# Running the first half of the wide matmul ahead of the small projection, and storing from GpSimd instead of ScalarE

## The chip, the cores and the metric

The kernel runs on one Trainium2 chip, on 8 cores. Each core handles one batch element of the input on its own: no data passes between cores. The metric is the device time of the slowest core in microseconds (us), lower is better.

## The reference, cut to what matters

For each batch element `x` is 4096 x 2048 in float32. `S` is 64.

```
xn = layernorm(x)                                # per row of 2048
a  = tanh(xn @ Wa.T + ba);  b = tanh(xn @ Wb.T + bb)      # 4096 x 64 each
h_t = a_t * h_(t-1) + b_t                        # scan over the 4096 rows
attn = xn + hs @ Wout.T + bout
scale = mean(|weight|)
w_t   = clip(round(weight / scale), -1, 1)       # 2048 x 2048, three values
ffn   = xn @ (w_t * scale).T + bias
y     = x + attn + ffn
```

## The kernel before, in words

A first stage (until about 174 us) prepares the weights. It loads the 2048 x 2048 matrix once to find its scale and again to make its three-valued form, turned by TensorE into `w_rhs` in bfloat16, and turns the two small projections into `wab` (128 columns: 64 for a, 64 for b).

Then comes the main loop over `NT` = 32 tiles of 128 rows, which has all that the change touches. There is no planner; each engine has a program written out by hand and meets the others by semaphores only. Buffers of a tile (`sx`, `xnb`, `xnT`, `outb`, `vv`) are doubled, but the accumulator `pffn` (128 x 2048 in float32, filled in four parts of 512 columns), the transpose buffer `ptr` and the small accumulator `pab` are single. For tile k:

- TensorE (the `tensor` block) computes `pab`: one bias matmul (L510) and 16 matmuls of 128 columns (L515). The first 8 need the first half of `xnT` and the last 8 its second half. It then waits until the first half of `pffn` of tile k-1 has been evicted (`s_ev` at 2k-1) and runs 32 matmuls of 512 columns for the first half of `pffn` (L527, L530). After `s_ev` at 2k it runs 32 more for the second half (L538, L542). Next are 16 transposes of tile k+1 from `xnb` into `ptr` (L552, L557), and four matmuls of `hsbe` with `wocv` that add the recurrent part to `pffn` (L566 to L572, below called the mix). The second and the fourth of the mix release the two evictions by `s_mix`.
- ScalarE (`scalar`) waits for both evictions of tile k-1 (`s_ev` at 2k) and issues the store of its `outb` (L263). It waits for `pab`, applies tanh to its two halves (L271, L272), makes `xnb` of tile k+1 (L281), scales the scan's result into `hsbe` (L290), and copies the transposes in two halves from `ptr` to `xnT` (L299, L303). The last store is L307.
- VectorE (`vector`) runs the scan (L394), copies its last column, makes the sums and sums of squares of tile k+2 (L371, L373), evicts the two halves of `pffn` into `outb` (L405, L411), and makes `vv` of tile k+1 (L421). L405 also waits for the store that last read its `outb` buffer, that of tile k-2.
- GpSimd (`gpsimd`, POOL in the rows) runs `chain(j)` for each tile: some twenty small operations (L601 to L633) that turn the sums into the row's scale and shift, `s_stats`, released by the drain of L635.
- SyncE (`sync`) loads `sx` of tile k+2 (L192) when `xnb` and `vv` of tile k have been made from it.

The order on TensorE around the change, as the code has it:

```python
                for c in range(NCH):
                    if c == 8:
                        tensor.wait_ge(s_xnT, 2 * k + 2)
                    ins = tensor.matmul(pab[:, :],
...
                ins.then_inc(s_ab, 1)
                if k == 0:
                    tensor.wait_ge(s_wtrc, 32)
                else:
                    tensor.wait_ge(s_ev, 2 * k - 1)
```

Of the kernel before, what the change touches and what calls it, by code (L numbers as in the profile page):

```python
# [15 lines left out]
T, D, S = 4096, 2048, 64  # L16
TT = 128
NT = T // TT
NCH = D // 128
# [6 lines left out]
def build():  # L26
# [12 lines left out]
    y_d = nc.dram_tensor("y", [T, D], F32, kind="ExternalOutput").ap()  # L39

    with ExitStack() as est:
# [9 lines left out]
        wab = sb("wab", [128, NCH * 128], BF16)  # L51
        wocv = sb("wocv", [65, D], BF16)
        hsbe = sb("hsbe", [65, TT], BF16)
        babr = sb("babr", [1, 128], BF16)
        sidn = sb("sidn", [128, 128], BF16)
        sonr = sb("sonr", [1, 128], BF16)
        sx = sb("sx", [128, 2 * D], F32)
        xnb = sb("xnb", [128, 2 * D], BF16)
        xnT = sb("xnT", [128, 2 * D], BF16)
        outb = sb("outb", [128, 2 * D], F32)  # L60
# [46 lines left out]
        pab = e(nc.psum_tensor("pab", [128, 128], F32))  # L107
        spare = e(nc.psum_tensor("spare", [128, 512], F32))
        s_x0, s_x1 = sem("s_x0"), sem("s_x1")
        s_st0, s_st1 = sem("s_st0"), sem("s_st1")  # L110
# [7 lines left out]
        s_small = sem("s_small")  # L118
# [5 lines left out]
        s_wabcp = sem("s_wabcp")  # L124
        s_bab = sem("s_bab")
# [71 lines left out]
        def _(scalar):  # L197
# [60 lines left out]
            scalar.drain()  # L258
            scalar.copy(xnT[:, 1024:2048], ptr[:, 1024:2048]).then_inc(s_xnT, 1)
            for k in range(NT):  # L260
                if k >= 1:
                    scalar.wait_ge(s_ev, 2 * k)
                    scalar.dma_start(  # L263
                        out=y_d[128 * (k - 1):128 * k, :],
                        in_=outb[:, ((k - 1) % 2) * D:((k - 1) % 2 + 1) * D]
                    ).then_inc(s_st[(k - 1) % 2], 16)
                scalar.wait_ge(s_ab, k + 1)
                if k >= 1:
                    scalar.wait_ge(s_scan, k)
                scalar.drain()  # L270
                scalar.activation(sa[:, :], pab[0:64, :], AF.Tanh)  # L271
                scalar.activation(sb0[:, :], pab[64:128, :], AF.Tanh  # L272
                                  ).then_inc(s_tanh, 2)
                if k < NT - 1:
                    j = k + 1
                    jsl = j % 2
                    scalar.wait_ge(s_stats, j + 1)
                    if k >= 1:
                        scalar.wait_ge(s_tr, 2 * k)
                    scalar.drain()  # L280
                    scalar.activation(xnb[:, jsl * D:(jsl + 1) * D],  # L281
                                      sx[:, jsl * D:(jsl + 1) * D], AF.Identity,
                                      bias=nmr[:, jsl:jsl + 1],
                                      scale=yr[:, jsl:jsl + 1]
                                      ).then_inc(s_xnbs, 1)
                scalar.wait_ge(s_scan, k + 1)
                if k >= 1:
                    scalar.wait_ge(s_mix, 2 * k)
                scalar.drain()
                scalar.activation(hsbe[0:64, :], hs[:, :], AF.Identity,  # L290
                                  bias=0.0, scale=invs64[:, :]).then_inc(s_hsb, 1)
                if k < NT - 1:
                    j = k + 1
                    jsl = j % 2
                    scalar.wait_ge(s_tr, 2 * k + 3)
                    if k >= 1:
                        scalar.wait_ge(s_ffn, k)
                    scalar.drain()
                    scalar.copy(xnT[:, jsl * D:jsl * D + 1024],  # L299
                                ptr[:, 0:1024]).then_inc(s_xnT, 1)  # L300
                    scalar.wait_ge(s_tr, 2 * k + 4)
                    scalar.drain()  # L302
                    scalar.copy(xnT[:, jsl * D + 1024:jsl * D + 2048],  # L303
                                ptr[:, 1024:2048]).then_inc(s_xnT, 1)

            scalar.wait_ge(s_ev, 2 * NT)
            scalar.dma_start(  # L307
                out=y_d[128 * (NT - 1):128 * NT, :],
                in_=outb[:, ((NT - 1) % 2) * D:((NT - 1) % 2 + 1) * D]
            ).then_inc(s_st[(NT - 1) % 2], 16)  # L310
            scalar.wait_ge(s_st0, 16 * ((NT + 1) // 2))
            scalar.wait_ge(s_st1, 16 * (NT // 2))

        @block.vector
        def _(vector):
# [112 lines left out]
        def _(tensor):  # L428
# [71 lines left out]
            for k in range(NT):  # L500
                ksl = k % 2
                xo = ksl * D
                if k >= 1:
                    tensor.wait_ge(s_tanh, 2 * k)
                else:
                    tensor.wait_ge(s_bab, 1)
                    tensor.wait_ge(s_wabcp, 2)
                    tensor.wait_ge(s_small, N_SMALL)
                tensor.wait_ge(s_xnT, 2 * k + 1)
                tensor.matmul(pab[:, :], babr[:, :], sonr[:, :],  # L510
                              start=True, stop=False)
                for c in range(NCH):
                    if c == 8:
                        tensor.wait_ge(s_xnT, 2 * k + 2)
                    ins = tensor.matmul(pab[:, :],  # L515
                                        wab[:, 128 * c:128 * (c + 1)],
                                        xnT[:, xo + 128 * c:xo + 128 * (c + 1)],
                                        start=False, stop=(c == NCH - 1))
                ins.then_inc(s_ab, 1)
                if k == 0:  # L520
                    tensor.wait_ge(s_wtrc, 32)
                else:
                    tensor.wait_ge(s_ev, 2 * k - 1)
                for c in range(NCH):
                    st_ = (c == 0)
                    lhs = xnT[:, xo + 128 * c:xo + 128 * (c + 1)]
                    tensor.matmul(pffn[:, 0:512],  # L527
                                  lhs, w_rhs[:, 2048 * c:2048 * c + 512],
                                  start=st_, stop=False)
                    tensor.matmul(pffn[:, 512:1024],  # L530
                                  lhs, w_rhs[:, 2048 * c + 512:2048 * c + 1024],
                                  start=st_, stop=False)
                if k >= 1:
                    tensor.wait_ge(s_ev, 2 * k)
                for c in range(NCH):
                    st_ = (c == 0)
                    lhs = xnT[:, xo + 128 * c:xo + 128 * (c + 1)]
                    tensor.matmul(pffn[:, 1024:1536],  # L538
                                  lhs,
                                  w_rhs[:, 2048 * c + 1024:2048 * c + 1536],  # L540
                                  start=st_, stop=False)
                    ins = tensor.matmul(  # L542
                        pffn[:, 1536:2048], lhs,
                        w_rhs[:, 2048 * c + 1536:2048 * c + 2048],
                        start=st_, stop=False)
                ins.then_inc(s_ffn, 1)
                if k < NT - 1:
                    j = k + 1
                    jo = (j % 2) * D
                    tensor.wait_ge(s_xnbs, j + 1)  # L550
                    for c in range(8):
                        ins = tensor.transpose(  # L552
                            ptr[:, 128 * c:128 * (c + 1)],
                            xnb[:, jo + 128 * c:jo + 128 * (c + 1)], sidn[:, :])
                    ins.then_inc(s_tr, 1)
                    for c in range(8, 16):
                        ins = tensor.transpose(  # L557
                            ptr[:, 128 * c:128 * (c + 1)],
                            xnb[:, jo + 128 * c:jo + 128 * (c + 1)], sidn[:, :])
                    ins.then_inc(s_tr, 1)  # L560
                tensor.wait_ge(s_hsb, k + 1)
                if k == 0:
                    tensor.wait_ge(s_wocp, 1)
                    tensor.wait_ge(s_cvr, 16 * 16)
                    tensor.wait_ge(s_hrow, 1)
                tensor.matmul(pffn[:, 0:512], hsbe[:, :], wocv[:, 0:512],  # L566
                              start=False, stop=True)
                tensor.matmul(pffn[:, 512:1024], hsbe[:, :], wocv[:, 512:1024],  # L568
                              start=False, stop=True).then_inc(s_mix, 1)
                tensor.matmul(pffn[:, 1024:1536], hsbe[:, :], wocv[:, 1024:1536],  # L570
                              start=False, stop=True)
                tensor.matmul(pffn[:, 1536:2048], hsbe[:, :], wocv[:, 1536:2048],  # L572
                              start=False, stop=True).then_inc(s_mix, 1)

        @block.gpsimd
        def _(g):
# [59 lines left out]

            chain(0)
            chain(1)
            for k in range(2, NT):
                chain(k)  # L640
            g.wait_ge(s_st0, 16 * ((NT + 1) // 2))
            g.wait_ge(s_st1, 16 * (NT // 2))

# [30 lines left out]
```

## Time and profile before

| what | us |
|---|---|
| median of the runs (2 runs, 739.09 to 740.08) | 739.59 |
| the profiled execution, its own time | 739.52 |
| its span, slowest core (core 5) | 737.9 |
| spans of the other cores | 732.8 to 736.9 |
| TensorE busy in the span | 590.1 |
| VectorE, ScalarE, GpSimd busy | 348.9, 235.9, 195.0 |

The span runs from the first to the last instruction of a core; the execution's own time is 1.6 us longer than the slowest span. Matmuls are pipelined: a matmul of 512 columns is shown as 0.38 us long but the next begins 0.22 us after it, so TensorE is read by the distance from one start to another. "PEld" is the loading of a matmul's fixed operand, which goes on beside the matmul before it. The suffix q (ACTq, SPq, POOLq) means an engine's queue of instructions that are not computation, such as the issue of a DMA.

### The profile page before, as it was taken

What the parts mean: (1) busy time and instruction counts of PE and PEld (TensorE: products, weight loads), DVE (VectorE), ACT (ScalarE), POOL (GpSimd) and SP (SyncE); (2) the same over time, 40 slices, a digit from 0 to 9 for tenths busy, and PEclk for the clock granted to TensorE, in tenths of its full rate; (3) what the DMA queues carried; (4) which work ended last, traced back from release to release, by engine and by line L of the source; (5) the groups of instructions that cost most, each with busy time, mean ns of one, the idle gap of its engine ahead of it and who ended that gap; (6) DMA issues with size and microseconds to landing.
All of it is one profiled execution on the core that took longest, in us unless ns stands there. A gap on an engine that the chain in (4) does not pass through costs nothing.

```text
span 737.9 us, 11312 instructions; the slowest of 8 cores (732.8 to 737.9 us)
## 1 busy us (share of the span) xinstructions
PE 590.1 (80%) x3804; PEld 312.0 (42%) x3804; DVE 348.9 (47%) x303; ACT 235.9 (32%) x250; POOL 195.0 (26%) x710
## 2 busy tenths in 40 slices
PE   0021244435999999999999999999999999999996
PEld 0021234323444444445444444444444445444442
DVE  0000099982344455554555554444455555555521
ACT  1275444533223222222332322233222222332320
POOL 1000022354222222222333333322222222323310
PEclk9999999999999999999999999999999999999998
DMA  8979557711244333333333344344333333333321
GB/s 231 297 234 334 189 170 258 258 56 58 69 129 139 123 115 115 115 115 115 115 115 114 124 138 137 126 133 136 122 116 114 115 115 115 115 115 115 122 84 81
DMA packets 17072, 103.03 MB, mean 140 GB/s; under 512 B 4566, under 2 KB 4598, under 8 KB 4598
## 3 DMA queue, kind: packets, MB, share of 16 engines
q1 hardware_dynamic: 9590, 51.96, 22.4%
q10 hardware_dynamic: 4608, 33.56, 12.7%
q0 software_dynamic: 2816, 16.78, 6.9%
q8 instruction: 31, 0.51, 0.3%
q14 instruction: 27, 0.22, 0.1%
HBM read 68.73 MB, written 33.55 MB: 139 GB/s over the span
## 4 chain that ended last, share of the span: by engine, by line
PE 64%; DMA 9%; ACT 8%; DVE 4%; DVEq 4%; ACTq 4%; issue 3%; SPq 2%; POOLq 1%; POOL 0%
PE pffn L527 15%; PE pffn L530 15%; PE pffn L538 15%; PE pffn L542 15%; ACT xnT L303 4%; DMA wtile<-wf 4%; DVE wbn L359 3%; ACTq L302 3%; PE pab L515 3%; DMA outb<-wf 2%; DMA wasb<-wb 2%; PE ptr L552 2%; DVEq L358 2%; SPq L171 2%; ACT xnT L232 2%
## 5 line engine op out<-in xcount | busy, mean ns | idle before, releaser
L527 PE MATMUL pffn<-w_rhs,xnT 128*128 128x512 bf16 x512 | 194.7, 380 | 0.6 <-DVE outb L405 0.6
L530 PE MATMUL pffn<-w_rhs,xnT 128*128 128x512 bf16 x512 | 194.6, 380 | 0.0
L538 PE MATMUL pffn<-w_rhs,xnT 128*128 128x512 bf16 x512 | 194.0, 379 | 0.0
L542 PE MATMUL pffn<-w_rhs,xnT 128*128 128x512 bf16 x512 | 194.0, 379 | 0.0
L371 DVE TENSOR_REDUCE sums<-sx 128x1 f32<-128x2048 f32 x32 | 73.2, 2286 | 191.0 <-DMA sx<-x 190.8
L281 ACT ACTIVATE xnb<-sx,nmr,yr 128x2048 bf16<-128x2048 f32 x31 | 65.0, 2097 | 106.8 <-POOLq L635 106.7
L299 ACT COPY xnT<-ptr 128x1024 bf16<-128x1024 bf16 x31 | 31.4, 1013 | 203.3 <-PE ptr L552 203.3
L601 POOL TENSOR_SCALAR mm_<-sums 128x1 f32<-128x1 f32 x32 | 9.6, 300 | 286.9 <-DVE sqscr L373 278.6
L542 PEld LDWEIGHTS pffn<-w_rhs,xnT 128*128 128x128 bf16 x512 | 50.1, 98 | 60.4
L538 PEld LDWEIGHTS pffn<-w_rhs,xnT 128*128 128x128 bf16 x512 | 50.1, 98 | 60.4
L405 DVE SCALAR_TENSOR_TENSOR outb<-pffn,negs,vv 128x1024 f32<-128x1024 f32 x32 | 41.1, 1284 | 72.4 <-PE pffn L568 72.4
L527 PEld LDWEIGHTS pffn<-w_rhs,xnT 128*128 128x128 bf16 x512 | 50.2, 98 | 57.7 <-issue 1.4
L530 PEld LDWEIGHTS pffn<-w_rhs,xnT 128*128 128x128 bf16 x512 | 50.2, 98 | 57.0 <-issue 0.6
L373 DVE SCALAR_TENSOR_TENSOR sqscr<-sx 128x2048 f32<-128x2048 f32 x32 | 73.0, 2281 | 0.0
L485 PE MATMUL ptr<-sidn,wbn 128*128 128x128 bf16 x256 | 29.8, 309 | 35.4 <-DVE wbn L359 35.4
L515 PE MATMUL pab<-xnT,wab 128*128 128x128 bf16 x512 | 40.0, 222 | 10.1 <-ACT xnT L303 10.1
L421 DVE TENSOR_SCALAR vv<-sx,p1r,nmr 128x2048 f32<-128x2048 f32 x31 | 41.7, 1347 | 3.0
L243 ACT COPY w_rhs<-ptr 128x1024 bf16<-128x1024 bf16 x32 | 32.4, 1013 | 33.5 <-PE ptr L485 32.1
L485 PEld LDWEIGHTS ptr<-sidn,wbn 128*128 128x128 bf16 x256 | 26.0, 144 | 39.5 <-issue 39.5
L411 DVE SCALAR_TENSOR_TENSOR outb<-pffn,negs,vv 128x1024 f32<-128x1024 f32 x32 | 41.1, 1284 | 3.0
L585 POOL DMA_DIRECT2D outb<-wf x11 | 10.3, 932 | 118.2 <-DVE wbn L359 117.7
L454 PE MATMUL spare<-onescolb,xnT 128*128 128x1 bf16 x256 | 9.0, 165 | 39.1 <-ACT xnT L232 39.1
(100 smaller groups left out, 562.3 us busy)
## 6 DMA issues: line engine op xcount, KB each, us to landing
sx<-x SPq DMA_DIRECT2D x32, 1024.0 KB, 6.9
y<-outb ACTq DMA_DIRECT2D x32, 1024.0 KB, 5.2
outb<-wf POOLq DMA_DIRECT2D x11, 1024.0 KB, 7.1
wtile<-wf SPq DMA_DIRECT2D x8, 1024.0 KB, 11.0
vv<-wf SPq DMA_DIRECT2D x8, 1024.0 KB, 10.5
sqscr<-wf POOLq DMA_DIRECT2D x5, 1024.0 KB, 7.3
wasb<-wa SPq DMA_DIRECT2D x1, 512.0 KB
wosb<-wout SPq DMA_DIRECT2D x16, 32.0 KB, 10.3
```

The costliest lines, as they stand in the source:

```text
L281: scalar.activation(xnb[:, jsl * D:(jsl + 1) * D], sx[:, jsl * D:(jsl + 1) * D], AF.Identity, bias=nmr[:, jsl:jsl + 1], scale=yr[:, jsl:js ...
L371: vector.reduce_sum(sums[:, jsl:jsl + 1], sx[:, jsl * D:(jsl + 1) * D], axis=AX.X)
L373: vector.scalar_tensor_tensor(sqscr[:, :], sx[:, jsl * D:(jsl + 1) * D], 1.0, sx[:, jsl * D:(jsl + 1) * D], OP.mult, OP.mult, accum_out=sq ...
L405: vector.scalar_tensor_tensor(outb[:, ksl * D:ksl * D + 1024], pffn[:, 0:1024], negs128[:, :], vv[:, ksl * D:ksl * D + 1024], OP.mult, OP. ...
L411: vector.scalar_tensor_tensor(outb[:, ksl * D + 1024:ksl * D + 2048], pffn[:, 1024:2048], negs128[:, :], vv[:, ksl * D + 1024:ksl * D + 2048],
L421: vector.tensor_scalar(vv[:, jsl * D:(jsl + 1) * D], sx[:, jsl * D:(jsl + 1) * D], p1r[:, jsl:jsl + 1], nmr[:, jsl:jsl + 1], OP.mult, OP.a ...
L485: ins = tensor.transpose(ptr[:, 128 * c:128 * (c + 1)], wbn[:, sl * D + 128 * c:sl * D + 128 * (c + 1)], sidn[:, :])
L515: ins = tensor.matmul(pab[:, :], wab[:, 128 * c:128 * (c + 1)], xnT[:, xo + 128 * c:xo + 128 * (c + 1)], start=False, stop=(c == NCH - 1))
L527: tensor.matmul(pffn[:, 0:512], lhs, w_rhs[:, 2048 * c:2048 * c + 512], start=st_, stop=False)
L530: tensor.matmul(pffn[:, 512:1024], lhs, w_rhs[:, 2048 * c + 512:2048 * c + 1024], start=st_, stop=False)
L538: tensor.matmul(pffn[:, 1024:1536], lhs, w_rhs[:, 2048 * c + 1024:2048 * c + 1536], start=st_, stop=False)
L542: ins = tensor.matmul(pffn[:, 1536:2048], lhs, w_rhs[:, 2048 * c + 1536:2048 * c + 2048], start=st_, stop=False)
```

## The change

Three edits in the main loop.

1. On TensorE the 32 matmuls for the first half of `pffn` go ahead of the 17 for `pab`. The wait for the eviction (`s_ev` at 2k-1) and that for `xnT` now stand before these 32, and the wait for the second half of `xnT` is at their channel 8. The 17 of `pab` come between the first and the second half of `pffn`.
2. ScalarE no longer waits for the evictions and no longer issues the stores, nor does it wait for them at the end.
3. GpSimd issues them: after `chain(k + 2)` it waits for both evictions of tile k and issues the store of tile k.

```diff
@@ scalar
             for k in range(NT):
-                if k >= 1:
-                    scalar.wait_ge(s_ev, 2 * k)
-                    scalar.dma_start(
-                        out=y_d[128 * (k - 1):128 * k, :],
-                        in_=outb[:, ((k - 1) % 2) * D:((k - 1) % 2 + 1) * D]
-                    ).then_inc(s_st[(k - 1) % 2], 16)
                 scalar.wait_ge(s_ab, k + 1)
...
-            scalar.wait_ge(s_ev, 2 * NT)
-            scalar.dma_start(
-                out=y_d[128 * (NT - 1):128 * NT, :],
-                in_=outb[:, ((NT - 1) % 2) * D:((NT - 1) % 2 + 1) * D]
-            ).then_inc(s_st[(NT - 1) % 2], 16)
-            scalar.wait_ge(s_st0, 16 * ((NT + 1) // 2))
-            scalar.wait_ge(s_st1, 16 * (NT // 2))
@@ tensor
-                if k >= 1:
-                    tensor.wait_ge(s_tanh, 2 * k)
-                else:
-                    tensor.wait_ge(s_bab, 1)
-                    tensor.wait_ge(s_wabcp, 2)
-                    tensor.wait_ge(s_small, N_SMALL)
-                tensor.wait_ge(s_xnT, 2 * k + 1)
-                tensor.matmul(pab[:, :], babr[:, :], sonr[:, :],
-                              start=True, stop=False)
-                for c in range(NCH):
-                    if c == 8:
-                        tensor.wait_ge(s_xnT, 2 * k + 2)
-                    ins = tensor.matmul(pab[:, :],
-                                        wab[:, 128 * c:128 * (c + 1)],
-                                        xnT[:, xo + 128 * c:xo + 128 * (c + 1)],
-                                        start=False, stop=(c == NCH - 1))
-                ins.then_inc(s_ab, 1)
                 if k == 0:
                     tensor.wait_ge(s_wtrc, 32)
                 else:
                     tensor.wait_ge(s_ev, 2 * k - 1)
+                tensor.wait_ge(s_xnT, 2 * k + 1)
                 for c in range(NCH):
+                    if c == 8:
+                        tensor.wait_ge(s_xnT, 2 * k + 2)
...
+                if k >= 1:
+                    tensor.wait_ge(s_tanh, 2 * k)
+                else:
+                    tensor.wait_ge(s_bab, 1)
+                    tensor.wait_ge(s_wabcp, 2)
+                    tensor.wait_ge(s_small, N_SMALL)
+                tensor.matmul(pab[:, :], babr[:, :], sonr[:, :],
+                              start=True, stop=False)
+                for c in range(NCH):
+                    ins = tensor.matmul(pab[:, :],
+                                        wab[:, 128 * c:128 * (c + 1)],
+                                        xnT[:, xo + 128 * c:xo + 128 * (c + 1)],
+                                        start=False, stop=(c == NCH - 1))
+                ins.then_inc(s_ab, 1)
                 if k >= 1:
                     tensor.wait_ge(s_ev, 2 * k)
@@ gpsimd
             chain(0)
             chain(1)
-            for k in range(2, NT):
-                chain(k)
+            for k in range(NT):
+                if k < NT - 2:
+                    chain(k + 2)
+                ksl = k % 2
+                g.wait_ge(s_ev, 2 * k + 2)
+                g.dma_start(out=y_d[128 * k:128 * (k + 1), :],
+                            in_=outb[:, ksl * D:(ksl + 1) * D]
+                            ).then_inc(s_st[ksl], 16)
```

## Rows read from the trace of the kernel before

**Rows 1.** Spans and granted TensorE clock of the cores.
```profile
core 5: 737.9 us, clock 0.997
```

**Rows 2.** The page's busy times, and TensorE in 40 slices of the span.
```profile
PE 590.1 (80%) x3804; PEld 312.0 (42%) x3804; DVE 348.9 (47%) x303; ACT 235.9 (32%) x250; POOL 195.0 (26%) x710
...
PE   0021244435999999999999999999999999999996
```

**Rows 3.** Waits, whole span: engine line <- releaser: us in total, times, longest.
```profile
PE pab L515 <- ACT xnT L303: 10.1, 31, 0.3
```

**Rows 4.** Timeline, boundary from tile 18 to 19: start us, us, engine, line, operation [idle before].
```profile
505.22 0.61 PE L552 MATMUL ptr<-sidn,xnb 128*128 128x128 bf16 x8
...
506.02 1.01 ACT L299 COPY xnT<-ptr 128x1024 bf16<-128x1024 bf16 x1 [6.70 <-PE ptr L552]
...
506.33 0.38 PE L568 MATMUL pffn<-wocv,hsbe 65*128 65x512 bf16 x1
...
506.93 1.28 DVE L405 SCALAR_TENSOR_TENSOR outb<-pffn,negs,vv 128x1024 f32<-128x1024 f32 x1 [1.93 <-PE pffn L568]
...
507.18 0.21 PE L510 MATMUL pab<-sonr,babr 1*128 1x128 bf16 x1
...
507.32 0.62 PE L515 MATMUL pab<-xnT,wab 128*128 128x128 bf16 x8
...
508.26 0.61 PE L515 MATMUL pab<-xnT,wab 128*128 128x128 bf16 x8 [0.33 <-ACT xnT L303]
...
508.71 0.38 PE L527 MATMUL pffn<-w_rhs,xnT 128*128 128x512 bf16 x1
```

**Rows 5.** Timeline, one tile later: the same transposes.
```profile
522.52 0.61 PE L552 MATMUL ptr<-sidn,xnb 128*128 128x128 bf16 x8
```

**Rows 6.** Timeline, an earlier boundary, where the eviction came late.
```profile
265.06 1.28 DVE L405 SCALAR_TENSOR_TENSOR outb<-pffn,negs,vv 128x1024 f32<-128x1024 f32 x1
...
266.49 0.38 PE L527 MATMUL pffn<-w_rhs,xnT 128*128 128x512 bf16 x1 [0.57 <-DVE outb L405]
```

**Rows 7.** Timeline, the other engines about the boundary of rows 4.
```profile
500.50 2.29 DVE L371 TENSOR_REDUCE sums<-sx 128x1 f32<-128x2048 f32 x1 [5.97 <-DMA sx<-x]
...
505.64 0.22 POOL L601 TENSOR_SCALAR mm_<-sums 128x1 f32<-128x1 f32 x1 [9.14 <-DVE sqscr L373]
...
509.67 0.34 ACTq L263 DMA_DIRECT2D y<-outb  x1
509.69 1.35 DVE L421 TENSOR_SCALAR vv<-sx,p1r,nmr 128x2048 f32<-128x2048 f32 x1
...
510.21 0.27 ACT L271 ACTIVATE sa<-pab 64x128 f32<-64x128 f32 x1 [2.10 <-DVE outb L411]
...
511.12 0.33 SPq L192 DMA_DIRECT2D sx<-x  x1
511.13 0.48 DVE L394 TENSOR_TENSOR_SCAN hs<-sa,h_in,sb 64x128 f32<-64x128 f32 x1
...
513.62 0.19 POOL L633 TENSOR_TENSOR nmr<-mm_,yr 128x1 f32<-128x1 f32 x1
...
514.04 2.10 ACT L281 ACTIVATE xnb<-sx,nmr,yr 128x2048 bf16<-128x2048 f32 x1 [3.27 <-POOLq L635]
```

**Rows 8.** Loads of sx (L192): us from issue to landing.
```profile
DMA to landing us min/median/max: 6.3/6.9/9.0
```

**Rows 9.** Weight loads of the small projection, 300 to 730 us: busy, mean ns.
```profile
L515 PEld LDWEIGHTS pab<-xnT,wab 128*128 128x128 bf16 x395 | 22.6, 97 | 13.6 <-issue 11.7
```

**Rows 10.** The tail, and GpSimd's own DMA issues (ns min/median/max) and landings.
```profile
733.71 0.34 ACTq L307 DMA_DIRECT2D y<-outb  x1
...
L585 POOL DMA_DIRECT2D outb<-wf x11: 528/947/1525, 1.7 to 144.4; - x11
...
DMA to landing us min/median/max: 6.4/7.1/14.1
```

**Rows 11.** Timeline of TensorE at tile 0, after a long idle time.
```profile
176.64 1.91 PE L515 MATMUL pab<-xnT,wab 128*128 128x128 bf16 x16
```

## The prediction, made before the change was run

> **What bounds the kernel now.** I read the spans first: the slowest core is core 5, at full TensorE clock [rows 1], and the others are alike, so one core tells all. The busy times and the slices come next: TensorE is at 9 tenths in every slice of the main loop and nothing else is near it [rows 2]. The question is thus only what TensorE does in one tile and where it stands still. The transposes of two successive tiles start at 505.22 and 522.52 [rows 4, 5]: a period of 17.30 us. Of that, from 508.71 to 522.52, 13.81 us go to the 64 wide matmuls, 0.216 each without a hole. The rest, from 505.22 to 508.71, is the boundary: 3.49 us. I read the boundary in the timeline, since all that the change moves ends there.
>
> In the boundary [rows 4] the 16 transposes and two matmuls of the mix are started by 506.33. That releases the eviction L405 (506.93 to 508.21). Beside it ScalarE copies the transposes (L299 from 506.02 to 507.03, then L303). The bias matmul L510 starts 0.15 us after the first copy ends, the first 8 of `pab` at 507.32; the next 8 wait 0.33 us for the second copy and start at 508.26. The waits show this 31 times, 10.1 us in total [rows 3]. The wide matmuls start at 508.71, when `pab` is through. The eviction had then been done for 0.5 us. So today the 17 matmuls of `pab` are what fills TensorE while it could not start the wide ones anyway: all but the last stretch of them lies in the shadow of L405.
>
> **TensorE: the wide half first.** What it saves is the start of the wide matmuls. They now need the first half of `xnT` (507.03) and the eviction L405 (508.21). The eviction is later and so it decides. How long after it TensorE starts is shown at one earlier boundary, where the eviction happened to be late: L405 from 265.06, so until 266.34, and the first wide matmul at 266.49 [rows 6]: 0.15 us. After the change the wide matmuls thus start at 508.36 in place of 508.71. Saved: 0.35 us for each boundary. Their channel 8 comes 16 matmuls or 3.4 us later, long after the second copy, so that wait costs nothing.
>
> What it costs: the 17 matmuls of `pab` no longer lie in a wait but in the stream of wide ones, with TensorE already full. In a stream they take their distance from one start to the next: from 508.26 to 508.71 eight of them take 0.45 us, 0.056 each [rows 4]. The 16 transposes with as many columns take the same (505.22 to about 506.11, when the mix begins 0.22 before L568). So 17 x 0.056 = 0.96 us. The lower bound is 0.94 (0.89 us for 16 transposes, scaled to 17); the upper is 1.05, if the bias matmul keeps the 0.14 us between it and the next (507.18 to 507.32) in place of 0.056. I take 0.96, as its weight load can go beside the wide matmul ahead of it.
>
> In sum for each boundary: 0.96 - 0.35 = +0.61 us, between 0.56 (0.94, and 0.03 us less delay after the eviction) and 0.70. The period becomes 17.91. There are 31 boundaries: +18.9 us, between 17.4 and 21.7. At tile 0 there is no eviction to wait for, and before and after TensorE does the same matmuls without a hole: 0. At the one boundary of rows 6 the eviction alone held the wide matmuls back, by about 0.4 us; with the better cover computed below that goes: -0.4 us.
>
> The page "TensorE: Matmul & The Clock Gate" of the Trainium skill (section "Back-to-back issue gap") puts matmuls of 128 columns, each with a weight load, at about 81 ns sustained rather than 56. By it the block would be an estimated 1.38 us and the whole some 13 us slower than my sum. This trace has 56 ns for just these matmuls [rows 4], and I go by it.
>
> **What gets late by it.** I count from the first wide matmul of a tile, t = 0, so that the eviction L405 before it ends at -0.15. `pab` is now complete at about t = 6.9 + 0.96 + 0.17 = 8.0 rather than before 0. Before, L271 started 2.10 us late, behind the eviction and the store issue, and the scan came 0.92 us after it (510.21 and 511.13) [rows 7]; now tanh starts at about 8.2 and the scan at 9.1 to 9.6, its column copy by 9.9. `xnb` of the next tile waited for GpSimd's chain (at 514.04, t = 5.3) and now for tanh: 8.8 to 10.9, and `hsbe` to 11.4. The transposes need `xnb` at 14.8 and the mix needs `hsbe` at 15.7. Both are covered, by 3.9 and 4.3 us.
>
> On VectorE the sums start when `sx` has landed or the scan is done. Load: L421 ends 511.04 and SyncE issues at 511.12 [rows 7], which in the new count is t = 2.76; at the median landing of 6.9 us [rows 8] that is 9.7, against 9.9 for the scan. The sums take 4.5 us and L405 follows 0.1 later. L405 is due at 14.77 (64 wide and `pab`) + 1.71 (505.22 to 506.93) = 16.5. So a landing may take up to 9.1 us, where it was 8.5 before; the longest seen is 9.0 [rows 8]. The cover of the sums becomes a little better, not worse.
>
> **Stores.** ScalarE loses its wait for both evictions and a 0.34 us issue, none of it on the path: ScalarE stood idle for 3.3 us ahead of L281 and now waits for `pab` in any case. I put it at nothing. GpSimd issues the store after the chain. The chain starts 0.64 us after the sums end and took 8.2 us (505.64 to 513.8) [rows 7], so the store is issued at about t = 5.3 of the next tile instead of 0.96. The next chain starts 0.6 us after the next sums, at about 15, so the issue (0.95 us [rows 10]) holds up nothing. The buffer is written again two tiles after its eviction, over 30 us later: nothing. Only the last store is on the path. Before, it was issued at 733.71 and the span ended at 737.9, 4.2 us. GpSimd's issue is 0.6 us longer than ScalarE's (0.947 against 0.34), and its 1 MB loads landed at best 6.4 us after issue [rows 10], but with other transfers beside them. Bounds: 0 and +2.8 (0.6, and 6.4 - 4.2). I take +1.0, nearer to the bare issue since the last store runs alone.
>
> The Trainium skill's page "DMA: Bandwidth & Descriptors" (section "Specifications") gives a first byte after about 1 us from GpSimd and 0.6 from the other queues. By it the tail would be an estimated 0.4 us longer, inside my bounds.
>
> **Sum.** Against the profiled execution's 739.5 us: +18.9 - 0.4 + 1.0 = +19.5, so 759.0 us. The median shown is 739.6, the same to 0.1. That is 2.6% slower.
>
> **Rivals.**
> A. The wide matmuls start before the eviction's time (the other side: faster). The mechanism: L405 ends ahead of the copy, so that only `xnT` at 507.03 holds TensorE. The wide matmuls then start at 507.18, a gain of 1.53 against 0.96: -0.57 for 31 boundaries, -17.7, plus the tail: 723. It decides from an L405 that ends before about 507.6 (508.71 - 0.96 - 0.15); at that point the change is worth nothing. Against it: L405 begins 0.22 after the mix matmul it needs, L568, has ended, and nothing of the change moves L568 nearer. For it I find no row. 0.02.
> B. The eviction holds less than I think, and the loss is about 0.4 a boundary: 739.5 + 31 x 0.4 + 1 = 753, within 2%. It would need the block at 0.8 us or a start 0.2 earlier. No row shows either. 0.05.
> C. The block costs more: in the stream the weight loads of `pab` are not hidden. One load takes 97 ns [rows 9]; 17 in full would be 1.65 us, +1.30 a boundary, 780. For it: the wide matmuls leave each load 216 ns, the narrow ones 56. Against it: the eight at 508.26 went at 0.056 with the same loads. 0.03. The skill's 81 ns, told above, would lie between.
> D. `sx` comes too late. The store now goes out inside the load's flight (5.3 in 2.8 to 9.7) instead of ahead of it, from a queue that shows landings of 7.1 us [rows 10]. The price is one for one beyond 9.1 us: with a median landing of 10, +0.9 x 31 = 28 us, so 787. Against it: before, a store as long as the last one (4.2) already lay beside the load for some 3 us (0.96 + 4.2 against the load's 2.4); now the load has its first 2.5 us to itself. 0.04.
> E. TensorE's clock falls in the longer hole. Its standstill at the boundary grows from two holes of 0.1 and 0.3 us to one of 1.2 us (L568 at 506.33 and two more at 0.216 and 0.38 long end at 507.14; to 508.36). After the long idle time ahead of tile 0, 16 matmuls of `pab` took 1.91 us, at the 1.2 GHz level, twice their time [rows 11]. If each boundary brought some 3 us of loss, +90: 850. No hole as long as 1.2 us lies in the main loop of before, so this stays open; the short ones that are there leave the pace untouched. 0.01.
>
> **How the numbers follow.** My forecast has 0.85. The range of its own terms is 756.5 (17.4, -0.4, 0) to 764.4 (21.7, 0.4 of rows 6 not recovered, 2.8). Taking in the edge of B and part of C, the range is 755 to 766. A measurement of this kernel tells about 2% from no change, 754.4 us here. Faster by over 2%: A, 0.02. Within 2%: B, 0.05. Slower by over 2%: 0.93.
>
> **What would show it.** In the changed kernel's timeline: the first L527 (new line) of a tile 0.15 us after L405 ends, released by VectorE in all 31 waits and no longer by ScalarE's L303; the second half's first matmul 0.96 us later than a wide matmul's pace would have it, the 17 of `pab` without a hole; transposes 17.9 us apart; L371 starting about 10 us after the first wide matmul; L405 still waiting for TensorE, not for the sums; the store issued by GpSimd about 5 us into the next tile; 5 us from the last issue to the end of the span. It is wrong if the period is below 17.75 or above 18.0, if L405 starts late behind L373, or if wide matmuls stand 0.43 us apart after a boundary.

## The result, and the profile of the changed kernel

The changed kernel takes 768.7 us (median) against 739.9 us for the kernel before on the same chips: a ratio of 1.0393, 95% interval 1.0376 to 1.041, so 3.9% slower. The forecast was slower too, but at 759.0 us with 766 as the upper end: the sign and the place are right, the size is a third too small. The profiled execution took 766.9 us, its slowest span is 765.4 us, against 739.5 and 737.9 before.

The changed kernel's page, the busy times and TensorE in slices:

```profile
PE 587.8 (77%) x3804; PEld 308.5 (40%) x3804; DVE 348.9 (46%) x303; ACT 235.6 (31%) x250; POOL 213.7 (28%) x742
...
PE   0121244409999899999999999999999998999995
```

The same work (587.8 us busy against 590.1 in [rows 2]) in a longer span: the loss is time in which TensorE stands still. The waits of the changed kernel's TensorE name it:

```profile
PE pffn L499 <- DVE outb L391: 41.1, 31, 1.4
```

L391 is the eviction of the first half (L405 before) and L499 the first wide matmul. In [rows 3] the boundary's only wait was for ScalarE's second copy, 0.33 us each, 10.1 in all, with `pab` around it. Now it is one wait of 1.3 us, 31 times, and nothing fills it. The timeline of the changed kernel from the middle of one tile to the start of the next:

```profile
504.75 0.38 PE L499 MATMUL pffn<-w_rhs,xnT 128*128 128x512 bf16 x1 [1.33 <-DVE outb L391]
...
511.44 0.38 PE L502 MATMUL pffn<-w_rhs,xnT 128*128 128x512 bf16 x1
511.75 0.22 PE L511 MATMUL pab<-sonr,babr 1*128 1x128 bf16 x1
511.91 1.07 PE L514 MATMUL pab<-xnT,wab 128*128 128x128 bf16 x16
512.81 0.38 PE L524 MATMUL pffn<-w_rhs,xnT 128*128 128x512 bf16 x1
...
519.72 0.61 PE L538 MATMUL ptr<-sidn,xnb 128*128 128x128 bf16 x8
...
520.83 0.38 PE L554 MATMUL pffn<-wocv,hsbe 65*128 65x512 bf16 x1
...
521.43 1.28 DVE L391 SCALAR_TENSOR_TENSOR outb<-pffn,negs,vv 128x1024 f32<-128x1024 f32 x1 [2.20 <-PE pffn L554]
...
522.97 0.38 PE L499 MATMUL pffn<-w_rhs,xnT 128*128 128x512 bf16 x1 [1.33 <-DVE outb L391]
```

The period is 522.97 - 504.75 = 18.22 us, where [rows 4, 5] had 17.30 and the prediction 17.91. Two places hold the missing 0.31:

- The wide matmul starts 0.26 us after the eviction has ended (521.43 + 1.28 = 522.71), not the 0.15 of [rows 6]. That is +0.11.
- From the last wide matmul of the first half, at 511.44, plus its 0.216, to the first of the second half at 512.81 `pab` takes 1.15 us, not 0.96. The 16 matmuls run at 0.056 (511.91 to 512.81), as foretold. The rest is at the one bias matmul, L511: it starts 0.31 after the wide one instead of 0.22, and the next starts 0.16 after it instead of 0.06. That is +0.19.

The weight loads about the bias matmul, in the same timeline, show how it differs from the others:

```profile
511.23 0.10 PEld L502 LDWEIGHTS pffn<-w_rhs,xnT 128*128 128x128 bf16 x1
...
511.75 0.09 PEld L511 LDWEIGHTS pab<-sonr,babr 1*128 1x128 bf16 x1 [0.42 <-issue]
...
511.90 0.90 PEld L514 LDWEIGHTS pab<-xnT,wab 128*128 128x128 bf16 x16
```

A wide matmul's load runs 0.2 us ahead of its matmul, beside the one before: the load of L502 at 511.23, the matmul at 511.44. L511's load comes only with its own matmul, and so does the first load behind it.

The whole difference adds up. From the first wide matmul of tile 1 to that of tile 31 (30 periods) it was 519.8 us before and is 546.5 now: +26.7. From there to the end of the span it was 21.6 and is 23.8: +2.2, which is the `pab` block (1.15) and the tail (+1.06). Ahead of tile 1 it is 1.4 less: this core came into the loop 0.65 earlier; tile 0 took 0.54 less (18.41 between the transposes of tile 0 and tile 1, before 18.95), which is told at the end; and the first boundary, from the transposes to the wide matmul, took 0.24 less (3.19, before 3.43). Sum +27.5, as 765.4 - 737.9.

### The profile page after: what moved, and what is told of

It is laid out like the page before. It is cut to its first block, busy times and chain, and to the rows that moved or that the text cites. A ratio compares the mean times of both kernels' runs of the same rounds, so it can differ in the third digit from the quotient of the medians.

```text
span 765.4 us, 11310 instructions; the slowest of 8 cores (761.0 to 765.4 us)
## 1 busy us (share of the span) xinstructions
PE 587.8 (77%) x3804; PEld 308.5 (40%) x3804; DVE 348.9 (46%) x303; ACT 235.6 (31%) x250; POOL 213.7 (28%) x742
## 3 DMA queue, kind: packets, MB, share of 16 engines
q0 software_dynamic: 7424, 50.34, 17.3%
## 4 chain that ended last, share of the span: by engine, by line
PE 70%; DVE 8%; DMA 7%; DVEq 5%; issue 3%; SPq 2%; ACT 2%; POOLq 1%; ACTq 1%; POOL 0%
PE pffn L499 15%; PE pffn L502 15%; PE pffn L528 14%; PE pffn L524 14%; DVE outb L391 5%; PE pab L514 4%; DMA vv<-wf 4%; DVE wbn L345 2%; DVEq L344 2%; DVEq L339 2%; PE ptr L538 2%; PE ptr L543 2%; DMA wasb<-wb 2%; SPq L171 2%; ACT xnT L232 1%
## 5 line engine op out<-in xcount | busy, mean ns | idle before, releaser
L499 PE MATMUL pffn<-w_rhs,xnT 128*128 128x512 bf16 x512 | 194.6, 380 | 41.6 <-DVE outb L391 41.1
L502 PE MATMUL pffn<-w_rhs,xnT 128*128 128x512 bf16 x512 | 194.6, 380 | 0.0
L380 DVE TENSOR_TENSOR_SCAN hs<-sa,h_in,sb 64x128 f32<-64x128 f32 x32 | 15.2, 476 | 219.8 <-ACT sb L266 219.8
L499 PEld LDWEIGHTS pffn<-w_rhs,xnT 128*128 128x128 bf16 x512 | 50.1, 98 | 113.4 <-issue 57.0
L265 ACT ACTIVATE sa<-pab 64x128 f32<-64x128 f32 x32 | 8.7, 271 | 280.7 <-PE pab L514 280.7
L391 DVE SCALAR_TENSOR_TENSOR outb<-pffn,negs,vv 128x1024 f32<-128x1024 f32 x32 | 41.1, 1284 | 77.3 <-PE pffn L554 77.3
L502 PEld LDWEIGHTS pffn<-w_rhs,xnT 128*128 128x128 bf16 x512 | 50.1, 98 | 57.1 <-issue 0.8
L611 POOL TENSOR_SCALAR t0s<-t0s 128x1 f32<-128x1 f32 x96 | 41.3, 431 | 15.3 <-issue 15.3
L571 POOL DMA_DIRECT2D outb<-wf x11 | 10.1, 920 | 117.6 <-DVE wbn L345 117.2
L397 DVE SCALAR_TENSOR_TENSOR outb<-pffn,negs,vv 128x1024 f32<-128x1024 f32 x32 | 41.1, 1284 | 3.0
```

The costliest lines, as they stand in the source:

```text
L391: vector.scalar_tensor_tensor(outb[:, ksl * D:ksl * D + 1024], pffn[:, 0:1024], negs128[:, :], vv[:, ksl * D:ksl * D + 1024], OP.mult, OP. ...
L397: vector.scalar_tensor_tensor(outb[:, ksl * D + 1024:ksl * D + 2048], pffn[:, 1024:2048], negs128[:, :], vv[:, ksl * D + 1024:ksl * D + 2048],
L499: tensor.matmul(pffn[:, 0:512], lhs, w_rhs[:, 2048 * c:2048 * c + 512], start=st_, stop=False)
L502: tensor.matmul(pffn[:, 512:1024], lhs, w_rhs[:, 2048 * c + 512:2048 * c + 1024], start=st_, stop=False)
L611: g.tensor_scalar(t0s[:, :], t0s[:, :], -0.5, 1.5, OP.mult, OP.add)
```

## The experiments

Every ratio is to runs of the kernel before on the same chip.

### Which of the two edits: e1 and e2

e1 has the new order on TensorE with the stores left on ScalarE; e2 has the stores on GpSimd with the old order.

```diff
 e1: the hunk of TensorE alone
 e2: the hunks of ScalarE and GpSimd alone
```

> Only the TensorE edit; the stores stay on ScalarE. If the order on TensorE carries all of it: a period between the transposes of 18.2 us, as in the changed kernel, and a time about 1 us below the changed kernel's 768 (the tail of a GpSimd store goes). Rival, that the stores on GpSimd cost part of each tile: a period clearly below 18.2 and a time below 765. Third possibility: ScalarE's wait for both evictions and its issue now delay tanh or xnb; they should not, since pab is complete only 8 us into the tile.

> Only the stores move to GpSimd; TensorE keeps the order of before. My theory: period 17.30 as before, time before + 1 us (tail only), so a ratio of 1.001. If the stores from GpSimd disturb the loads of sx: landings of sx above 7 us and late evictions. If they help (in the changed kernel the loads land in 5.6 us and never late): landings near 5.6 to 6 and the one late boundary gone, -0.4 us.

e1: ratio 1.0408 (1.0386 to 1.043), 770.5 us. e2: ratio 1.0025 (1.001 to 1.0039), 742.5 against 740.2 us. Two successive groups of transposes, first of e1, then of e2:

```profile
507.06 0.61 PE L552 MATMUL ptr<-sidn,xnb 128*128 128x128 bf16 x8
...
525.28 0.61 PE L552 MATMUL ptr<-sidn,xnb 128*128 128x128 bf16 x8
```

```profile
505.71 0.61 PE L538 MATMUL ptr<-sidn,xnb 128*128 128x128 bf16 x8
...
523.00 0.61 PE L538 MATMUL ptr<-sidn,xnb 128*128 128x128 bf16 x8
```

Periods of 18.22 and 17.29: the order on TensorE carries the whole loss of each tile, the stores none of it. e1 did not come out 1 us below the changed kernel, as I had expected, because its slowest core entered the loop late (transposes of tile 0 at 178.15, in the changed kernel's profile 173.51). From there to the end e1 takes 591.8 us and the changed kernel 591.9. That these two are alike is chance: e1's first period is 0.85 us longer (19.26 against 18.41), and from its last transposes to the end it is 1.02 us shorter (743.88 to 769.9, against 738.36 to 765.4). So the tail of a GpSimd store does cost 1 us. e2 says the same from the other side: 26.1 us from the last transposes to the end, 25.1 in the kernel before.

In e2 the loads of `sx` land in a median of 5.3 us on core 3, where the kernel before has 7.0. From 200 us on, the median is lower on every core: 5.1 to 6.3 us, before 6.2 to 7.0. The page of e2 gives:

```profile
sx<-x SPq DMA_DIRECT2D x32, 1024.0 KB, 5.3
y<-outb POOLq DMA_DIRECT2D x32, 1024.0 KB, 5.8
```

So the later store does not hold up the load; its landings are shorter. Nothing on the path waits for it, so it does not show in the time.

### The start after the eviction: e3

```diff
-                if k == 0:
-                    tensor.wait_ge(s_wtrc, 32)
-                else:
-                    tensor.wait_ge(s_ev, 2 * k - 1)
                 tensor.wait_ge(s_xnT, 2 * k + 1)
+                if k == 0:
+                    tensor.wait_ge(s_wtrc, 32)
+                else:
+                    tensor.wait_ge(s_ev, 2 * k - 1)
```

> The changed kernel, with the two waits ahead of the first wide matmul in the other order: that for xnT (long satisfied) first, that for the eviction last. Theory that the second wait instruction is passed only after the first is released, and costs about 0.11 us: the first wide matmul starts 0.15 us after the eviction's end instead of 0.26, period 18.11, time 31 x 0.11 = 3.4 us below the changed kernel. Rival, that a stalled TensorE simply needs 0.26 us after VectorE: no difference.

Ratio 1.0349 (1.0318 to 1.0381). Its waits, and its timeline from one group of transposes to the next:

```profile
PE pffn L499 <- DVE outb L391: 37.6, 31, 1.2
```

```profile
500.67 0.61 PE L538 MATMUL ptr<-sidn,xnb 128*128 128x128 bf16 x8
...
502.38 1.28 DVE L391 SCALAR_TENSOR_TENSOR outb<-pffn,negs,vv 128x1024 f32<-128x1024 f32 x1 [2.19 <-PE pffn L554]
...
503.81 0.38 PE L499 MATMUL pffn<-w_rhs,xnT 128*128 128x512 bf16 x1 [1.22 <-DVE outb L391]
...
518.77 0.61 PE L538 MATMUL ptr<-sidn,xnb 128*128 128x128 bf16 x8
```

The wide matmul now starts 0.15 us after the eviction's end (502.38 + 1.28 = 503.66), as in [rows 6]. The period is 18.10, 0.12 less, and the wait went from 41.1 to 37.6 us over 31 boundaries, 0.11 each. So the order of two waits matters although the second has been satisfied long before: the wait behind the one that holds the engine is passed only after it, for 0.11 us. The satisfied one ahead costs nothing. The time alone, 765.9 us, would have shown this only weakly; the rows show it at each boundary.

### The bias matmul: e4 and e5

e4 gives the bias matmul 128 rows (the biases in one, zeros in 127, against ones) and leaves everything else:

```diff
-        babr = sb("babr", [1, 128], BF16)
+        babr = sb("babr", [128, 128], BF16)
...
-        sonr = sb("sonr", [1, 128], BF16)
+        sonr = sb("sonr", [128, 128], BF16)
...
+            vector.memset(babr[:, :], 0.0)
+            vector.memset(sonr[:, :], 1.0)
```

> The changed kernel, with the bias matmul of pab on 128 rows (one row of biases, 127 rows of zeros) instead of 1 row; the same result and the same count of matmuls. Theory that the one-row matmul is what breaks the stream (holes of 0.09 us ahead of it and 0.10 behind it): the pab block goes from 1.15 to 0.96 us, period 18.03, time 31 x 0.19 = 5.9 us below the changed kernel. Rival, that the hole ahead of it comes from the wait for tanh that stands there: only the hole behind goes, 31 x 0.10 = 3.1 us.

e5 leaves the bias matmul on one row and moves the wait for tanh, which stood right ahead of it, to the head of the tile:

```diff
+                if k >= 1:
+                    tensor.wait_ge(s_tanh, 2 * k)
...
-                if k >= 1:
-                    tensor.wait_ge(s_tanh, 2 * k)
                 tensor.matmul(pab[:, :], babr[:, :], sonr[:, :],
```

> The changed kernel, with the wait for tanh moved from just ahead of the bias matmul to the head of the tile (it is long satisfied at both places). Theory: the holes about the bias matmul come from its one-row shape alone, as e4 says; the bias matmul still starts 0.31 us after the last wide one and the next 0.16 after it, but one more wait now stands ahead of the eviction's, which is passed early: period 18.22 unchanged. Rival, that the wait for tanh makes the first of the two holes: the bias matmul starts 0.22 after, period 18.12.

e4: ratio 1.0327 (1.0295 to 1.036), 765.6 us. Its timeline:

```profile
504.18 0.61 PE L543 MATMUL ptr<-sidn,xnb 128*128 128x128 bf16 x8
...
514.33 0.22 PE L516 MATMUL pab<-sonr,babr 128*128 128x128 bf16 x1
514.38 1.06 PE L519 MATMUL pab<-xnT,wab 128*128 128x128 bf16 x16
...
522.18 0.61 PE L543 MATMUL ptr<-sidn,xnb 128*128 128x128 bf16 x8
```

The next matmul starts 0.05 after the bias, and the period is 18.00 here and 18.01 in the median: 0.21 less, near the 0.19 expected. The time alone would have misled: 765.6 is 3.1 us below the changed kernel's 768.7, which is what the rival had said. The profiled core came into the loop late (transposes of tile 0 at 178.46), and one of its periods is 20.08 us long. That long one has something that the changed kernel's slowest core never shows behind a boundary. Here it is, first in the timeline, then in the windows view, whose last three numbers are the granted clock, the DMA share and GB/s:

```profile
433.70 0.38 PE L504 MATMUL pffn<-w_rhs,xnT 128*128 128x512 bf16 x1 [1.71 <-DVE outb L396]
```

```profile
434.66:437.65 2.99, 2.99 (x9) 1.03 (x7) 1.51 (x2) 0.00 (x0) 2.19 (x6) 0.50 0.10 16
```

The eviction began 0.38 us later than elsewhere, for a cause that stays open (e6 has one such boundary too, without what follows). After this longer wait the granted clock fell to 0.50, the 1.2 GHz level, and the wide matmuls stood 0.43 apart. That cost 1.7 us.

e5, a single run of 767.4 us, has the holes where they were:

```profile
511.90 0.38 PE L508 MATMUL pffn<-w_rhs,xnT 128*128 128x512 bf16 x1
512.21 0.23 PE L511 MATMUL pab<-sonr,babr 1*128 1x128 bf16 x1
512.37 1.07 PE L514 MATMUL pab<-xnT,wab 128*128 128x128 bf16 x16
```

0.31 and 0.16 again, with no wait between. So the wait is not the cause and the one-row matmul is. In the changed kernel its load isn't taken ahead, nor is the load behind it; in e4 the bias matmul's load starts at 514.11, 0.22 us ahead of its matmul. Whether that lies in the one row of its weights or in that of its moving operand I did not separate; both have one row.

### Both terms together: e6

e6 has the edits of e3 and e4, and so behaves on TensorE as my prediction had assumed.

> The changed kernel with both e3's swap and e4's bias on 128 rows: what my prediction assumed for TensorE. If the two terms are all that it missed: the wide matmuls start 0.15 after the eviction, the pab block is 0.96, period 17.89 to 17.91, time 9 to 10 us below the changed kernel, so about 759 (ratio 1.026). Rival, that something else (the prologue, the tail, the stores) took part: a time above 762 with a period of 17.9.

Ratio 1.0281 (1.0251 to 1.0311), 759.9 us. Two boundaries of its timeline:

```profile
500.96 0.38 PE L504 MATMUL pffn<-w_rhs,xnT 128*128 128x512 bf16 x1 [1.22 <-DVE outb L396]
...
518.86 0.38 PE L504 MATMUL pffn<-w_rhs,xnT 128*128 128x512 bf16 x1 [1.22 <-DVE outb L396]
```

17.90, against the predicted 17.91. In a period, the two terms are all that the prediction missed. The time agrees less well than 759.9 beside 759.0 makes it look: this chip runs the kernel before in 738.4 us, so that the forecast's +19.5 would be 757.9 here, a ratio of 1.0264, which lies within the interval.

### Does the same edit help where pab stands in a wait: e7

```diff
 the kernel before, with e4's edit
```

> The kernel before, with the bias matmul on 128 rows as in e4. There the bias matmul stands in the boundary, in a wait: the first 8 of pab start some 0.09 us sooner after it, and the next 8 wait as long as before for the second copy. So if only what stands in TensorE's stream costs time, the 0.19 us that the same edit gave in the changed kernel give nothing here: period 17.30, ratio 1.000. Rival, that the edit is worth its 0.09 to 0.19 us wherever pab stands: 3 to 6 us, ratio 0.992 to 0.996.

Ratio 1.0003 (0.9991 to 1.0015): nothing. Its timeline shows why:

```profile
505.99 0.61 PE L557 MATMUL ptr<-sidn,xnb 128*128 128x128 bf16 x8
...
507.94 0.22 PE L515 MATMUL pab<-sonr,babr 128*128 128x128 bf16 x1
508.00 0.61 PE L520 MATMUL pab<-xnT,wab 128*128 128x128 bf16 x8
509.03 0.61 PE L520 MATMUL pab<-xnT,wab 128*128 128x128 bf16 x8 [0.42 <-ACT xnT L305]
...
523.28 0.61 PE L557 MATMUL ptr<-sidn,xnb 128*128 128x128 bf16 x8
```

The first 8 come 0.09 us sooner after the bias, and the wait for the second copy grows from 0.33 to 0.42. In a wait an instruction is free, in a stream it has its full price. This is the change's own mechanism, seen from the other side: it moved `pab` from the first place to the second.

### A version that is faster than both: v1, v2 and e8

If what stands in the boundary's shadow is free, the better course is to leave no boundary. v1 keeps `pab` where it was before and moves what makes TensorE wait. The first two mix matmuls go between the two wide halves, so that the first eviction runs beside the second half; so do the transposes of the next tile, so that the copies do. The bias has 128 rows. In outline:

```diff
                 ...   # pab, then the first wide half, as before
+                tensor.wait_ge(s_hsb, k + 1)
+                tensor.matmul(pffn[:, 0:512], hsbe[:, :], wocv[:, 0:512], ...)
+                tensor.matmul(pffn[:, 512:1024], hsbe[:, :], wocv[:, 512:1024], ...).then_inc(s_mix, 1)
+                if k < NT - 1:
+                    ...   # the 16 transposes of tile k + 1
                 ...   # the second wide half
-                if k < NT - 1:
-                    ...   # the 16 transposes of tile k + 1
-                tensor.wait_ge(s_hsb, k + 1)
-                tensor.matmul(pffn[:, 0:512], hsbe[:, :], wocv[:, 0:512], ...)
-                tensor.matmul(pffn[:, 512:1024], hsbe[:, :], wocv[:, 512:1024], ...).then_inc(s_mix, 1)
                 ...   # the mix of the second half
```

> The kernel before, with pab still ahead of the wide matmuls, the bias on 128 rows, and on TensorE the first two mix matmuls and then the transposes of the next tile moved between the two wide halves. The first eviction then runs beside the second wide half, so the boundary has neither L405 nor the copies to wait for. If TensorE's stream alone sets the time: period 13.81 + 0.96 + 0.89 + 0.86 = 16.5 to 16.6, time before - 31 x 0.75 - 1.4 (one eviction less at the end) = about 715. Rival: VectorE's sums of tile k+2, which wait for the load of sx until some 9 us into the tile, come so late that the eviction behind them (done at 15.3 at best) holds the next wide matmuls in some tiles: period 16.6 to 17, time 716 to 730.

Ratio 0.9969 (0.9937 to 1.0002): no gain that can be told from none (734.4 us in the profiled execution). Neither side of what I expected came true. The evictions did not hold the wide matmuls; something else did, as its waits on TensorE and its timeline show:

```profile
PE pffn L543 <- ACT hsbe L292: 16.1, 16, 2.5
```

```profile
503.92 0.22 POOL L606 TENSOR_SCALAR mm_<-sums 128x1 f32<-128x1 f32 x1 [8.59 <-DVE sqscr L378]
...
510.08 0.33 SPq L194 DMA_DIRECT2D sx<-x  x1
...
511.92 0.19 POOL L638 TENSOR_TENSOR nmr<-mm_,yr 128x1 f32<-128x1 f32 x1
...
512.34 2.09 ACT L283 ACTIVATE xnb<-sx,nmr,yr 128x2048 bf16<-128x2048 f32 x1 [2.60 <-POOLq L640]
514.52 0.40 ACT L292 ACTIVATE hsbe<-hs,invs 64x128 bf16<-64x128 f32 x1
...
515.06 0.38 PE L543 MATMUL pffn<-wocv,hsbe 65*128 65x512 bf16 x1
...
516.18 2.29 DVE L376 TENSOR_REDUCE sums<-sx 128x1 f32<-128x2048 f32 x1 [5.37 <-DMA sx<-x]
```

`hsbe` is wanted 8 us earlier than before, and on ScalarE it stands behind `xnb`, which stands behind GpSimd's 8 us chain, which stands behind the sums, which wait for the load; and the load is issued only after `vv`, the last thing VectorE does in a tile. The chain that ended last has DMA at 21% and GpSimd's queue at 12% on v1's page; in the kernel before it was 9% and 1%. These steps form a ring, since the load in turn starts from `xnb` and `vv`. In a period of 17.3 us the ring had time to spare; with `hsbe` wanted 8 us earlier it has none. From 201.4 to 703.1 us v1's 29 periods are together 22.4 us longer than 16.53 each. The waits for `hsbe` make 19.1 of it. The other 3.3 are two stretches behind such waits (2.27 and 2.11 us long), where the granted clock was 0.50.

v2 breaks the ring: VectorE makes `vv` of tile k+1 right after the scan, ahead of the sums of tile k+2, not after the evictions.

```diff
                 vector.tensor_copy(h_in[:, 0:1], hs[:, TT - 1:TT])
+                if k < NT - 1:
+                    ...   # wait s_stats at k + 2, make vv of tile k + 1
                 if k < NT - 2:
                     sums_sqs(k + 2)
                 ...   # the two evictions
-                if k < NT - 1:
-                    ...   # wait s_stats at k + 2, make vv of tile k + 1
```

> v1, and on VectorE the making of vv of tile k+1 moved ahead of the sums of tile k+2, so that sx is free, and loaded again, some 14 us earlier. TensorE then never waits for the load: period 16.5, time 714 to 716 on all cores. If v1 is already free of waits for the load, v1 and v2 are equal within 0.2%.

714.2 us, ratio 0.9659 (0.9639 to 0.968): 3.4% faster than the kernel before and 7% faster than the changed one. Its timeline, one boundary:

```profile
501.17 0.61 PE L552 MATMUL ptr<-sidn,xnb 128*128 128x128 bf16 x8
...
509.19 0.38 PE L577 MATMUL pffn<-wocv,hsbe 65*128 65x512 bf16 x1
509.41 0.22 PE L515 MATMUL pab<-sonr,babr 128*128 128x128 bf16 x1
509.47 1.05 PE L520 MATMUL pab<-xnT,wab 128*128 128x128 bf16 x16
510.36 0.38 PE L532 MATMUL pffn<-w_rhs,xnT 128*128 128x512 bf16 x1
...
517.70 0.61 PE L552 MATMUL ptr<-sidn,xnb 128*128 128x128 bf16 x8
```

No hole is left: a period of 16.53, which is the sum of TensorE's own pieces (13.81 wide, 0.96 `pab`, 0.89 transposes, 0.86 mix). In the windows view the stretch from 200 to 700 us has TensorE busy for 500.00 us of 500; the kernel before had 489.02. The 31 periods give 31 x 0.77 = 24 us, what the time shows.

e8 is v2 with the bias back on one row.

> v2 with the bias matmul back on one row. Here pab stands in a full stream with the mix (65 rows) ahead of it. If the one-row matmul breaks any full stream: period 16.52 + 0.19 = 16.71, time about 714 + 6 = 720. If the hole ahead of it needs 128-row matmuls before it, less: 717.

Ratio 0.9744 (0.9724 to 0.9764). Against v2 that is 0.85 points, some 6.3 us. Its timeline:

```profile
515.68 0.38 PE L572 MATMUL pffn<-wocv,hsbe 65*128 65x512 bf16 x1
515.99 0.23 PE L510 MATMUL pab<-sonr,babr 1*128 1x128 bf16 x1
516.14 1.07 PE L515 MATMUL pab<-xnT,wab 128*128 128x128 bf16 x16
```

0.31 and 0.15, as in the changed kernel, and a period of 16.73 (transposes at 507.66 and 524.39). So one row costs 0.2 us in this full stream too, behind the mix as behind the wide matmuls: 6.3 us of v2's gain are the bias on 128 rows, the rest is the new order.

## Why the prediction was wrong in size

**The mechanism was right.** TensorE's order loses because `pab` leaves a wait that is there anyway and enters a full stream. The waits are released by VectorE 31 times in place of ScalarE, as the prediction asked; e1 and e2 show that nothing else takes part in a tile.

**The step that failed is the sum for each boundary**, "0.96 - 0.35 = +0.61 us, between 0.56 [...] and 0.70". It measured 18.22 - 17.30 = 0.92, outside the bounds, and the period passed the 18.0 that the prediction had named as a sign of being wrong. Both of its terms were off in the same direction:

- "So 17 x 0.056 = 0.96 us" measured 1.15. I had the number at hand: the bias matmul and the next stood 0.14 apart in [rows 4]. I took that for an effect of the wait before it and wrote that "its weight load can go beside the wide matmul ahead of it". It can't (e4, e5). Even the upper bound, 1.05, allowed only for the hole behind, not for the one ahead.
- The start 0.15 us after the eviction came from [rows 6], where one wait stood. The change puts a second wait behind it, which costs 0.11 (e3). I had read the added wait for `xnT` only for when it would be satisfied, and never priced the instruction.

With both taken away (e6) the ratio is 1.0281, where the forecast was 1.0264.

Two smaller slips did not decide. The late boundary of [rows 6] had cost 0.74 us (a period of 18.04 against 17.30), not 0.4. And the upper end of the forecast's own terms is 739.5 + 21.7 + 2.8 = 764.0, not 764.4.

**What held.** Without the two terms the period is 17.90 (17.91 foretold). In the changed kernel tanh starts 8.4 us into the tile (8.2), the sums at 10.0 (9.9), the store at 5.5 (5.3). The eviction waits for TensorE (2.2 us in most tiles), never for the sums, so the late boundary of [rows 6] is gone. That the better cover removed it isn't shown: e2, with the old order, doesn't have it either. The last store, from 760.62 to 765.4, with its issue 0.56 us after the eviction rather than 0.08, makes the tail 1.06 us longer (1.0).

**The rivals.** A did not come: L391 starts 0.60 after the mix matmul L554, exactly as before. B neither. C had the right address, the `pab` block's weight loads, but the wrong count: not 17 loads show, only the two about the one-row matmul. The Trainium skill's 81 ns a matmul ("TensorE: Matmul & The Clock Gate", section "Back-to-back issue gap") has no support here either: 16 in a stream went at 56 ns (511.91 to 512.81 in the changed kernel, 509.47 to 510.36 in v2). D went the other way: landings of 5.6 us on core 3, where the kernel before has 7.0 on that core, and none above 6.0. E did not come at the changed kernel's holes of 1.3 us: the wide matmuls behind them stand 0.216 apart at once, at the 2.4 GHz level. But its mechanism is real. The clock fell once behind a wait of 1.71 us (e4) and twice behind waits of 2.27 and 2.11 us (v1); it did not behind waits of 1.64 (e6) and 2.48 us (v1). Each fall cost 1.6 to 1.7 us, not the 3 of the prediction.

## What to carry to other kernels

Before moving work "out of the way" of an engine that is full, ask what it stands in now: in a wait that stays, it is free (e7, 1.000), in the stream it has its whole price (the change, +3.9%). The gain lies in moving the cause of the wait: here the eviction's last input and the transposes, placed between two halves (v2, -3.4%, of which 0.85 points are the bias on 128 rows), together with the slowest feedback ring behind them, which a shorter period lays bare (v1). Price each moved instruction from a stream of its own kind, the odd-shaped one by itself, and put the wait that will be the last to come true last.

## What was unexpected of the hardware

- A matmul with one row of weights and one of data in a stream of 128-row matmuls costs 0.2 us more than its 0.056: its weight load and the one behind it aren't taken ahead. Filled up with zero rows to 128 it is free of that (period 18.22 to 18.00 in the changed kernel, 16.73 to 16.53 in v2). The mix, on 65 rows, shows no such hole; row counts between 1 and 65 were not tried.
- A second wait instruction behind the one that holds TensorE costs 0.11 us, though satisfied (start 0.26 us after the eviction, 0.15 in e3); ahead of it, nothing (e3, and e5 with one more there).
- TensorE's clock fell behind three waits in the main loop (1.71 us in e4, 2.27 and 2.11 in v1) and not behind one of 2.48 us (v1). The granted clock was then 0.50, in e4 from 434.66 to 437.65 us.
- At tile 0 the matmuls go at the 1.2 GHz pace for a while (wide ones 0.43 apart), although the granted clock of the windows view is 1.00 there. From the transposes of tile 0 this lasts 5.9 us on the slowest core of the kernel before (174.16 to 180.05) and 4.4 on that of the changed kernel (173.51 to 177.90). That goes with the 0.54 us by which tile 0 is shorter there.
- The slowest core's arrival in the loop varies by more than most terms here: transposes of tile 0 between 167.0 and 178.5 us over the profiled executions and their cores. Differences under 5 us are better read from the period than from the time.
